# A new order for the first tile of a fused attention and feed-forward kernel, and four raw weight pieces in place of two

## The reference, cut to what matters

```python
# x, ctx: (8, 256, 256) float32; mask: (8, 256); w1, w2: (1024, 256); h1, h2: (1024, 1024); w3: (256, 1024)
scores = einsum('bqd,bkd->bqk', layernorm(x), ctx) / 16      # causal and key mask to -inf
x = x + softmax(scores) @ ctx
z = layernorm(x)
h = silu(z @ w1.T * s1) * (z @ w2.T * s2)
h = gelu(h @ h1.T * sh1)
h = gelu(h @ h2.T * sh2)
out = x + h @ w3.T * s3
```

## Time and profile before

| | us |
|---|---|
| median of 3 runs | 377.39 (375.11 to 377.93) |
| the profiled execution's own time | 376.71 |
| its span in the trace | 374.6 |
| PE busy in the span | 364.7 (97%) |
| first product of the feed-forward part | 20.31 |
| first product for batch 1 | 24.84 |
| all 22 pieces loaded and tested | 85.80 |

### The profile page before, as it was taken

How to read it: one execution, slowest core, us unless ns; L and a number is a source line. 1 busy time by engine, 2 the same in 40 slices (tenths; PEclk the granted TensorE clock), 3 DMA queues, 4 the chain that set the end, 5 groups by cost and what they waited for, 6 DMA issues and landing times.

```text
span 374.6 us, 4879 instructions
## 1 busy us (share of the span) xinstructions
PE 364.7 (97%) x1797; PEld 306.8 (82%) x1797; DVE 176.9 (47%) x406; ACT 149.3 (40%) x252; POOL 28.5 (8%) x50
## 2 busy tenths in 40 slices
PE   8898999999999999999998999999999999999996
PEld 5676888888898888888888888888889888888886
DVE  2747652334565745234564665232456563232324
ACT  3678766593134632262130653235113473122120
POOL 7300031000100022000010004000010000000000
PEclk9999999999999999999999999999999999999999
DMA  7989998981411000000141000000000100000001
GB/s 260 335 288 366 380 401 281 317 274 70 173 40 46 3 2 2 2 0 3 59 139 60 2 1 3 0 2 3 2 0 30 32 3 2 2 2 2 2 2 58
DMA packets 10499, 34.15 MB, mean 91 GB/s; under 512 B 1522, under 2 KB 4468, under 8 KB 10100
## 3 DMA queue, kind: packets, MB, share of 16 engines
q1 hardware_dynamic: 10448, 33.45, 24.9%
q10 hardware_dynamic: 4, 0.00, 0.0%
HBM read 31.34 MB, written 13.63 MB: 120 GB/s over the span
## 4 chain that ended last, share of the span: by engine, by line
PE 93%; issue 2%; ACT 1%; DVE 1%; POOL 1%; DMA 1%; DVEq 0%; ACTq 0%
PE ring L928 62%; PE ring L907 14%; PE ring L947 8%; PE att L858 2%; PE att L877 2%; PE att L848 1%; DMA mask<-in_mask 1%; ACT scaled L391 1%; PE ring L1073 1%; ACT gate L468 1%; PE att L866 1%; PE ring L1055 0%; ACT h_hi L458 0%; PE ring L1092 0%; POOL rstd L338 0%
## 5 line engine op out<-in xcount | busy, mean ns | idle before, releaser
L928 PE MATMUL ring<-h_hi,weights 128*128 128x512 f32 x512 | 201.5, 394 | 0.1
L928 PE MATMUL ring<-h_lo,weights 128*128 128x512 f32 x512 | 199.5, 390 | 0.0
L928 PEld LDWEIGHTS ring<-h_hi,weights 128*128 128x128 f32 x512 | 96.2, 188 | 19.9 <-issue 0.2
L928 PEld LDWEIGHTS ring<-h_lo,weights 128*128 128x128 f32 x512 | 96.2, 188 | 19.7
L480 ACT ACTIVATE act<-ring,scales 128x512 f32<-128x512 f32 x64 | 44.1, 689 | 155.8 <-PE ring L928 155.8
L716 DVE CAST h_hi<-act 128x512 fp32r<-128x512 f32 x64 | 27.3, 427 | 147.9 <-ACT act L480 134.1
L610 DVE TENSOR_TENSOR h_lo<-act,h_hi 128x512 fp32r<-128x512 f32 x96 | 66.2, 689 | 2.6
L907 PE MATMUL ring<-xn_hi,weights 128*128 128x512 f32 x112 | 43.7, 390 | 1.5 <-issue 1.5
L907 PE MATMUL ring<-xn_lo,weights 128*128 128x512 f32 x112 | 43.6, 389 | 0.0
L468 ACT ACTIVATE gate<-ring,scales 128x512 f32<-128x512 f32 x32 | 22.1, 690 | 37.6 <-PE ring L907 37.6
L703 DVE SCALAR_TENSOR_TENSOR act<-ring,scales,gate 128x512 f32<-128x512 f32 x32 | 24.0, 751 | 21.5 <-PE ring L907 17.0
(11 more groups left out here) (119 smaller groups left out, 243.5 us busy)
## 6 DMA issues: line engine op xcount, KB each, us to landing
weights_staged<-in_weights SPq DMA_DIRECT2D x22, 512.0 KB, 7.0
weights<-weights_staged SPq DMA_DIRECT2D x22, 512.0 KB, 5.6
x_in<-in_x SPq DMA_DIRECT2D x8, 256.0 KB, 2.9
ctx_cols<-in_ctx_cols SPq DMA_DIRECT2D x8, 256.0 KB, 4.3
ctx_rows<-in_ctx_rows SPq DMA_DIRECT2D x4, 512.0 KB, 6.3
out_dram<-residual SPq DMA_DIRECT2D x16, 128.0 KB, 2.2
mask<-in_mask SPq DMA_DIRECT2D x3, 256.0 KB
gate<-in_weights SPq DMA_DIRECT2D x1, 512.0 KB, 5.2
```

Of the source, the lines that this page charges most:

```text
L928: ins = nc.tensor.matmul(bank[:], w, part[:, k].bitcast(dt), start=(k == 0 and part is h_hi[src]), stop=(k == HC - 1 and part is h_lo[src]))
```

## The change

It does five things.

- The rows of tile 0 go in the order 0, 1, 2, 3 in place of 1, 0, 3, 2, and the hand-written order changes on PE, ACT, DVE and POOL with it.
- All four gate and up pieces come raw. Pieces 2 and 3 go into `ctx_cols` and `work`, so their DMAs wait on SP until tile 0's scores and turned probabilities are done with these tiles. They are no longer staged and loaded at the start; their staging goes behind pieces 11 and 12 and their loads behind piece 21.
- The three groups for gate and up become two (pieces 0 and 1; pieces 2 and 3), and seven branches become two.
- POOL copies piece 1 only when row 1 is normalised, and pieces 2 and 3 only when row 3 is; it takes the reciprocal root of rows 2 and 3 apart.
- The idle products are 14 of 256 columns and then 6, in place of 6 of 512 columns and then 1, 1 and 3.

```diff
--- before.py
+++ after.py
@@ -48,12 +48,11 @@
 HID2_CHUNKS = ((0, 3), (3, 5), (5, 8))
 
 
-GATE_UP_A, GATE_UP_B, GATE_UP_C, HID1A, HID1B, HID1C, HID2A, HID2B, LAST = range(9)
-FLAG_ENDS = (1, 2, 4, 7, 9, 12, 15, 17, PIECES)
+GATE_UP_A, GATE_UP_B, HID1A, HID1B, HID1C, HID2A, HID2B, LAST = range(8)
+FLAG_ENDS = (2, 4, 7, 9, 12, 15, 17, PIECES)
 FLAG_PIECES = tuple(zip((0, *FLAG_ENDS), FLAG_ENDS))
 RING = 6
 CH = 3 * HC
-FIRST_ROWS = (1, 0, 3, 2)
...
-        first_pieces = [h_hi[1][:, 2 * n:2 * n + 2].rearrange("p c t -> p (c t)") for n in range(2)]
-        raw_pieces = [gate[:].rearrange("p n t -> p (n t)"), residual[:].rearrange("p r d -> p (r d)")]
+        first_pieces = [h_hi[1][:, 2 * n:2 * n + 2].rearrange("p c t -> p (c t)") for n in range(GU_P)]
+        raw_pieces = [gate[:].rearrange("p n t -> p (n t)"), residual[:].rearrange("p r d -> p (r d)"),
+                      ctx_cols[:].rearrange("p b c t -> p (b c t)"), work[:]]
...
@@ -265,19 +265,23 @@
             load_queries(0)
             load_keys(0)
             sp.wait_ge(x_loaded[0], 16)
+            load_values(0)
             load_raw(0)
-            load_values(0)
             load_raw(1)
-            stage(2)
+            sp.wait_ge(first_scores[3], 1)
+            load_raw(2)
             sp.dma_start(scales[:], scales_d).then_inc(scales_in, 16)
-            stage(3)
+            stage(GU_P)
+            sp.wait_ge(first_probs_turned[3], 1)
+            load_raw(3)
+            stage(GU_P + 1)
             ahead = 2
 
-            for n in range(2, PIECES):
+            for n in range(GU_P, PIECES):
                 load_piece(n)
                 if n + ahead < PIECES:
                     stage(n + ahead)
-                if n in (FLAG_PIECES[HID1C][0], FLAG_PIECES[HID1C][0] + 1):
+                if FLAG_PIECES[HID1C][0] <= n < FLAG_PIECES[HID1C][0] + GU_P:
                     stage(n - FLAG_PIECES[HID1C][0])
                 if n == FLAG_PIECES[HID1A][0]:
                     sp.dma_start(down_scale[:], down_scale_d.partition_broadcast(P)).then_inc(down_scale_in, 16)
@@ -285,10 +289,11 @@
                     sp.wait_ge(x_attn_done, ROWS)
                     load_queries(1)
                 if n == FLAG_PIECES[HID1C][1] - 1:
+                    sp.wait_ge(hid_mm, 1)
                     load_keys(1)
                     load_mask(1)
                     load_values(1)
-            for n in range(2):
+            for n in range(GU_P):
                 load_piece(n)
             for t in range(TILES - 2):
...
 
             first_mask_of(0)
+            first_rstd_of(0)
             first_mask_of(1)
-            first_rstd_of((0, 1), 2)
-            first_rstd_of((2, 3), 4)
-            first_rstd_of((1,), 5)
+            first_rstd_of(1)
             first_weights(0)
-            first_rstd_of((0,), 6)
+            first_attention_rstd(0)
+            first_attention_rstd(1)
+            pool.wait_ge(first_xn[1], 1)
             first_weights(1)
-            first_rstd_of((2, 3), 8)
+            first_attention_rstd(2)
+            first_attention_rstd(3)
+            pool.wait_ge(first_xn[3], 1)
+            first_weights(2)
+            first_weights(3)
             for t in range(1, TILES):
...
@@ -504,27 +516,28 @@
             act.dma_start(mask[0:1, :, 0:SEQ].bitcast(I32), mask_d[0:1]).then_inc(mask_loaded, 16)
             act.wait_ge(down_free, ROWS)
             load_table(0, ACT.Exp)
-            first_deviation(1, 1)
-            first_deviation(0, 2)
+            first_deviation(0)
+            first_deviation(1)
+            first_queries(0)
+            first_deviation(2)
             first_queries(1)
-            first_queries(0)
-            first_deviation(2, 4)
-            first_queries(3)
+            first_queries(2)
+            first_exponentials(0)
             first_exponentials(1)
-            first_exponentials(0)
+            first_exponentials(2)
+            first_evacuate_probs(1)
+            first_evacuate_probs(2)
+            first_exponentials(3)
             test_piece(0, raw_pieces[0], raw_in[0])
-            first_exponentials(3)
+            test_piece(1, raw_pieces[1], raw_in[1])
             first_evacuate_probs(3)
-            first_exponentials(2)
-            first_evacuate_probs(2)
-            test_piece(1, raw_pieces[1], raw_in[1])
+            first_split(0)
             first_split(1)
-            first_split(0)
+            test_piece(2, raw_pieces[2], raw_in[2])
+            test_piece(3, raw_pieces[3], raw_in[3])
+            first_split(2)
+            first_split(3)
             load_table(1, ACT.Silu)
-            test_piece(2)
-            first_split(3)
-            first_split(2)
-            test_piece(3)
             act.wait_ge(scales_in, 16)
 
 
...
@@ -778,57 +793,52 @@
...
+            first_attention_stats(1)
+            first_moments_of(1, 1)
+            first_attention(2)
+            first_normalise(0)
+            first_normalise(1)
+            first_attention_stats(2)
             take_flag(GATE_UP_A)
-            first_normalise(1, 3)
-            first_inverse((2, 3), 2)
+            first_split(0)
+            first_split(1)
+            first_moments_of(2, 1)
             first_attention(3)
-            first_normalise(0, 4)
             first_attention_stats(3)
-            first_split(1)
-            first_attention(2)
-            first_moments_of(3, 7)
-            first_split(0)
-            first_attention_stats(2)
-            first_moments_of(2, 8)
-            take_flag(GATE_UP_B)
-            for r in (3, 2):
-                first_normalise(r, 5)
-            for r in (3, 2):
-                first_split(r)
+            first_moments_of(3, 1)
+            first_normalise(2)
+            first_normalise(3)
+            first_split(2)
+            first_split(3)
             dve.wait_ge(scales_in, 16)
             tile(0)
             for t in range(1, TILES - 1):
...
                 def piece(n):
-                    if t > 0 or n >= 2:
+                    if t > 0:
                         return weights[:, n]
                     return first_pieces[n] if dt == F32R else raw_pieces[n]
...
@@ -953,8 +963,6 @@
             def segment(flag, products):
 
                 pe.wait_ge(flag_ready, flag + 1)
-                if flag in (GATE_UP_A, GATE_UP_B):
-                    pe.wait_ge(first_copied, flag + 1)
                 value = pe.value_load(seg_flags[0:1, flag:flag + 1].bitcast(I32), min_val=0, max_val=2**31 - 1)
                 with pe.If(value == 0):
                     products(F32R)
@@ -969,20 +977,30 @@
                                  ).then_inc(flag_mm, 1)
 
             def first_tile():
-                gate_up = lambda flag, chunks, b=None: segment(flag, lambda dt: gate_and_up(0, chunks, dt, b))
+                def batches(dt):
+
+                    pe.wait_ge(first_copied, 1)
+                    gate_and_up(0, (0, 1), dt, 0)
+                    first_turn_xn(2)
+                    first_turn_xn(3)
+                    pe.wait_ge(first_copied, 2)
+                    gate_and_up(0, (2,), dt, 0)
+                    gate_and_up(0, (0,), dt, 1)
+                    sum_flag(GATE_UP_B)
+                    gate_and_up(0, (1, 2), dt, 1)
+                    gate_and_up(0, (3,), dt)
+
+                def remaining(dt):
+
+                    pe.wait_ge(first_copied, GU_P)
+                    gate_and_up(0, (4, 5), dt)
+                    sum_flag(HID1A)
+                    gate_and_up(0, (6, 7), dt)
+
                 hid1 = lambda flag, *chunks: segment(flag, lambda dt: hidden(0, 0, chunks, dt))
                 hid2 = lambda flag, *chunks: segment(flag, lambda dt: hidden(0, 1, chunks, dt))
-                gate_up(GATE_UP_A, (0, 1), 0)
-                first_turn_xn(3)
-                first_turn_xn(2)
-                gate_up(GATE_UP_B, (2,), 0)
-                gate_up(GATE_UP_A, (0, 1), 1)
-                gate_up(GATE_UP_B, (2,), 1)
-                sum_flag(GATE_UP_C)
-                gate_up(GATE_UP_B, (3,))
-                gate_up(GATE_UP_C, (4, 5))
-                sum_flag(HID1A)
-                gate_up(GATE_UP_C, (6, 7))
+                segment(GATE_UP_A, batches)
+                segment(GATE_UP_B, remaining)
                 hid1(HID1A, 0, 1)
                 sum_flag(HID1B)
                 hid1(HID1A, 2)
@@ -1044,7 +1062,8 @@
             def stay_busy(n):
 
                 for _ in range(n):
-                    nc.tensor.matmul(ring[RING - 1][:], h_lo[0][:, 0, 0:P], h_lo[0][:, 0], start=True, stop=True)
+                    nc.tensor.matmul(ring[RING - 1][:, 0:SEQ], h_lo[0][:, 0, 0:P], h_lo[0][:, 0, 0:SEQ], start=True,
+                                     stop=True)
 
             def first_turn(r):
 
@@ -1102,36 +1121,33 @@
                 ins.then_inc(first_xn_turned[r], 1)
 
             pe.wait_ge(idle_made, 1)
-            stay_busy(6)
+            stay_busy(14)
             pe.wait_ge(ident_made, 1)
```

(35 more changed lines are left out.)

107 lines of the change are left out of this document (52 added, 55 removed).

## The result

The changed kernel takes **380.1 us** (median of four runs, 378.63 to 382.3), the kernel before 376.7 in the four runs beside it: a ratio of 1.010, 95% interval 1.006 to 1.015. Forecast were 377.0 and at most 379.2.

What follows compares the result with a forecast made beforehand. PE was taken as busy nearly throughout, so only an earlier start of its products could pay. Batch 1's 1.7 us gain was lost to late pieces at `LAST`: sum 0.0, 376.7, forecast 377.0 by the median, range 374.8 to 379.2.

Steps and rivals of the forecast that it cites:

- the rest of the kernel (tiles 1 to 3) is unchanged: Everything after tile 0 was taken to run as before, at a cost of 0.
- The clock rival: PE stays at its lower clock longer at the front, through batch 0: 379.5 us, chance 0.05.
- First product 18.4: Tile 0's first feed-forward product starts at 18.4 us in place of 20.31, bounds 17.7 and 19.6.
- The port rule's 18.9: GpSimd and vector engine share a port pair, so the moved copy delays row 1's `first_neg_max` half a us: first product 18.9.
- Batch 1 at 23.1: Batch 1's products in tile 0 start at 23.1, 1.7 earlier than 24.84, after raw piece 3's 6.4 us transfer.
- the other end (22.3): If raw piece 3 took 3.2 us, batch 1 would follow batch 0 directly at 22.3, a gain of 2.5.
- The 3.2: Estimated transfer time of a 512 KB piece: 2.0 us plus its bytes over 436 GB/s.
- The piece chain, net 0.0: Later weight pieces in tile 0 shrink the front's 1.7 to 1.4 at piece 14 and to nothing at `LAST`.
- Staging price, 0 to 1.63 each: Stagings of pieces 2 and 3, moved into the queue, delay later pieces: 0.8 for piece 14, 1.65 for piece 21.
- Rival 1: The front's gain survives because the stagings go into DMA gaps: 1.6 us gained, 375.4, chance 0.24.
- rival 2: Slower through the piece chain: each staging costs its full 1.63, piece 21 is 3.8 late, 378.7 us, chance 0.20.

Runs made afterwards that it cites:

- the run with the late store: The changed kernel with SP waiting for the first gate product of tile 2 before it issues the four output stores of tile 1; 379.7 us, ratio 1.006.

## Why the prediction was wrong

- **The step that failed** is the sentence "the rest of the kernel (tiles 1 to 3) is unchanged". Its products and waits were, its place in the program wasn't: the term that I set to 0 measured +1.2 for the pause and +1.7 for the clock. With 2.9 the sum of 377.0 would have been 379.9, against 380.1 measured. The kernel before already had `202.14 1.09 issue` in its chain, a pause without a cause in the middle of steady work. I read the chain only over its first 60 us. I costed branches at the 0.46 of a register load each, and left the rule cited above out of the count.
- **The clock rival** had the low clock as a cost, but in the first 20 us. Its 2.5 more, near the 2.9 that was lost, is luck: the clock cost 1.7, and that behind the pause. The first 20 us do have a half-clock part of two lengths, in both kernels. The clock fell behind each of the three profiled pauses of 2.07, 2.31 and 2.82 us and behind none of the six of 1.10 or less. The length of a gap alone doesn't decide: in the run with the late store PE stood for 2.72 us before its product at 65.98, waiting for a piece's test, the windows from 62 to 70 us all read 1.00, and the products behind it take 0.40, no longer than usual:

```profile
65.98 0.35 PE L978 MATMUL att<-low_sums,ones 128*128 128x3 f32 x2 [2.72 <-ACT scaled L405]
```

- **First product 18.4:** 18.75, within its bounds; executions with an early start have it at 16.6 to 17.1, below them. The normalisations of rows 0 and 1 took 0.40 and 0.41 with no copy beside them, where in the kernel before the two took 1.10 and 1.03, each beside a POOL copy, so that term was right. The port rule's 18.9 can't be told from 18.75 by this number. The half us that the rule gave `first_neg_max(1)` isn't there: the copy ran at 9.68 for 1.03, so it ended just as `first_neg_max(1)` began at 10.71, 0.04 behind the end of the maximum that it needs, and that took 0.16. The two didn't overlap, so this doesn't test the rule.
- **Batch 1 at 23.1:** 22.52, nearer the other end (22.3). Raw piece 3, issued at 14.84, landed at 20.0 and so took 5.2, not 6.4; the gate of chunk 0 came 2.3 earlier. The 3.2 that the prediction took from the Trainium skill, page "DMA: Bandwidth & Descriptors", did not come either; the fit there is for transfers that GpSimd issues, and these are issued on SP.
- **The piece chain, net 0.0:** right in sum, since the two kernels stood within 0.15 us at 114 and at 202; over all profiles with a late start and two stagings, tile 1 begins at 114.0 to 114.8 in the changed kernel and at 113.6 to 114.5 in the kernel before. The place was wrong. Test 14 ended at 65.1 (forecast 64.6), but the gain was lost to test 12's wait of 5.79 and test 13's 1.89, not at `LAST`, where test 21 ended at 87.0 and the sum came at 87.90, 0.1 earlier than in the earlier trace rows. I put the price on pieces 14 and 21 and left out 12 and 13, which stand right behind the moved stagings.
- **Staging price, 0 to 1.63 each:** the wrong term. Moving all four away gave nothing, and a third staging under way brought tile 1 forward by 1.3 (early starts), which I never asked for.
- **Rival 1** came true only with three stagings (1.5 to 4 us, where it had 1.6), and **rival 2** has the right sign by another cause.

What stays open: why the changed kernel's pause is 2.1 to 2.8 us long where that of the kernel before is at most 1.1 at five places within 10 instructions of each other; the count from the compiled program doesn't bring them onto one curve. Open too is the second low stretch that the mean clocks of 0.991 and 0.990 in two of the changed kernel's runs suggest (one stretch makes 0.995). The 380.1 against 374.4 to 376.2 without the long pause is 4 to 6 us, of which the traces give 4.1 for a pause with low clock against none; the rest is within what two kinds of start and the other low stretch do to a median.

## What to carry to other kernels

Read the chain of waits to its end, and take each "issue" of a microsecond in steady work for a cost that any edit, even one before it, can double; runtime branches belong around whole stages and not around each group of products. When an edit starts the main engine earlier, ask what feeds it and how many transfers are under way, not only how full the DMA engines look. Before blaming an edit for a small loss, time it once with some never-executed code added to both versions. And compare two profiles only after seeing that the same products take the same time in their first microseconds.

## What the runs showed of the hardware

- Eight instructions that are never executed changed the changed kernel's time by 1% (ratio to before 1.010 without, 0.999 with them); between tiles 1 and 3 the profiles took 180.13 us without them and 177.17 with them, 175.99 with 64 of them.
- At the jump to tile 2, pauses of TensorE of 2.07, 2.31 and 2.82 us were followed by granted clock 0.50, for some 3.4 us in the changed kernel, and six of 0.36 to 1.10 were not. A wait of 2.72 us at 63 us, in the run with the late store, was not followed by it either.
- The same four passes near the start took 1.03 us in seven profiled executions and 1.69 to 1.91 in twelve, which moved the first feed-forward product of the changed kernel from 16.60 to 18.75.
- A normalisation on DVE of 128x256 took 1.03 and 1.10 us beside a POOL copy of 128x1024, and 0.40 and 0.41 without one.
- A DMA share of 1.00 went with 381 GB/s with two stagings of 512 KB under way and 1.02 with 421 with three, while the median transfer between 20 and 85 us took 5.5 us (loads) and 6.7 (stagings) with two and 7.5 and 9.3 with three.
